# Layers 2 and 3 of a four-layer graph network: attention applied to x first, then the product with W

## What is computed

```python
Wh = jnp.einsum('bnd,de->bne', x, W)
e_src = jnp.einsum('bnd,d->bn', Wh, a_src)
e_dst = jnp.einsum('bnd,d->bn', Wh, a_dst)
logits = e_src[:, :, None] + e_dst[:, None, :]
logits = jnp.where(logits >= 0, logits, 0.2 * logits)
attn = softmax(where(adj == 0, -inf, logits))
out = jnp.einsum('bnm,bmd->bnd', attn, Wh)
```

## Time and profile before

| | us |
|---|---|
| median of 3 runs | 3392.47 (3390.36 to 3393.50) |
| span of the profiled execution | 3390.5 |
| mean granted TensorE clock | 0.992 |
| layer 0 and layer 1, to the start of the last stage | about 2310 |
| last stage | about 1080 |

### The profile page before, as it was taken

How to read it: one execution, slowest core, us unless ns; L and a number is a source line. 1 busy time by engine, 2 the same in 40 slices (tenths; PEclk the granted TensorE clock), 3 DMA queues, 4 the chain that set the end, 5 groups by cost and what they waited for, 6 DMA issues and landing times. The chain is left out here.

```text
span 3390.5 us, 58748 instructions
## 1 busy us (share of the span) xinstructions
PE 3273.9 (97%) x16217; PEld 2651.5 (78%) x16217; DVE 2186.4 (64%) x4753; ACT 1691.7 (50%) x4193; POOL 1989.9 (59%) x2870
## 2 busy tenths in 40 slices
PE   8999989999999999999999999996999999999997
PEld 6777768888888888888888888885777777777775
DVE  6777655555555555555555555555778877877775
ACT  2111135555555555555555555543665666666665
POOL 4555564444444444444444444433888888888886
PEclk9999999999999999999999999998999999999999
DMA  4343310000000000000000000002111111111110
GB/s 140 118 127 126 94 47 16 19 19 19 19 19 19 19 19 19 19 19 19 19 19 19 19 19 19 19 25 90 41 47 56 46 46 56 46 46 50 52 46 28
DMA packets 76527, 143.98 MB, mean 42 GB/s; under 512 B 8640, under 2 KB 8640, under 8 KB 76480
## 3 DMA queue, kind: packets, MB, share of 16 engines
q1 hardware_dynamic: 73920, 135.07, 12.1%
q0 software_dynamic: 2560, 8.39, 0.9%
HBM read 93.09 MB, written 50.33 MB: 42 GB/s over the span
## 5 line engine op out<-in xcount | busy, mean ns | idle before, releaser
L715 POOL TENSOR_TENSOR w_first<-xin,v_row 128x512 f32<-128x512 f32 x512 | 719.9, 1427 | 493.6 <-ACT w_first L753 482.8
L845 DVE TENSOR_TENSOR hT_lo<-hv,hT_hi 128x512 fp32r<-128x512 f32 x256 | 296.7, 1159 | 428.8 <-ACT hT_hi L771 428.8
L47 PE MATMUL whp<-big_hi,xT_hi 128*128 128x512 f32 x1024 | 422.6, 413 | 0.0
L47 PE MATMUL wop<-big_hi,hT_hi 128*128 128x512 f32 x1024 | 405.2, 396 | 0.0
L47 PE MATMUL wop<-big_hi,hT_lo 128*128 128x512 f32 x1024 | 401.0, 392 | 0.0
L47 PE MATMUL whp<-big_lo,xT_hi 128*128 128x512 f32 x1024 | 401.0, 392 | 0.0
L47 PE MATMUL whp<-big_hi,xT_lo 128*128 128x512 f32 x1024 | 400.6, 391 | 0.0
L47 PE MATMUL wop<-big_lo,hT_hi 128*128 128x512 f32 x1024 | 398.7, 389 | 0.0
L767 ACT COPY wh<-whp 128x512 f32<-128x512 f32 x256 | 149.0, 582 | 384.3 <-PE whp L47 384.3
L1139 POOL TENSOR_TENSOR g_terms<-x,g_v_row 128x512 f32<-128x512 f32 x256 | 329.0, 1296 | 5.0 <-ACT x L1219 4.9
L753 ACT ACTIVATE w_first<-w_first 128x512 f32<-128x512 f32 x512 | 319.4, 627 | 5.1 <-POOL w_first L715 5.1
(11 more groups left out here) (200 smaller groups left out, 8018.8 us busy)
## 6 DMA issues: line engine op xcount, KB each, us to landing
xt<-in_x SPq DMA_DIRECT2D x64, 256.0 KB, 2.7
x_scratch<-x SPq DMA_DIRECT2D x64, 256.0 KB, 2.0
xin<-x_scratch SPq DMA_DIRECT2D x64, 256.0 KB, 2.6
att_scratch<-attT SPq DMA_DIRECT2D x64, 256.0 KB, 2.0
att<-att_scratch SPq DMA_DIRECT2D x64, 256.0 KB, 2.7
x1r<-x_scratch SPq DMA_DIRECT2D x64, 256.0 KB, 3.0
out<-res SPq DMA_DIRECT2D x64, 256.0 KB, 2.0
stage<-in_L_gnn_W_heads POOLq DMA_DIRECT2D x16, 256.0 KB, 2.9
```

The costliest lines, as they stand in the source:

```text
L47: ins = nc.tensor.matmul(out, a, b, start=first and c == 0 and q == 0, stop=last and c == n - 1 and q == 2)
L715: nc.gpsimd.tensor_tensor(terms[:, k % TR, :], xin[:], v_row[:, k, :], ALU.mult).then_inc(terms_ready, 1)
L845: nc.vector.tensor_tensor(hT[h % 2][1][:].rearrange("p c n -> p (c n)"), hv[h % 2][:], hT[h % 2][0][:].bitcast(F32).rearrange("p c n -> p ...
```

## The change

For layers 2 and 3, `turn_x`, `sums` and the copy `wh_out` go. `aggregate` takes their place: for each of four chunks of x, an fp32 matmul with the 128x128 chunk of x stationary and `turned` (128 columns) moving. This gives (attn @ x) already transposed, in the bank `agg`. ACT copies its high part (`agg_hi`), DVE makes the low part (`agg_lo`), and `project` multiplies with W and writes straight to `g.sums`, from which `residual` reads. `bank_a` goes, and each layer gets a PSUM bank of its own for scores and turned probabilities. The orders on PE, ACT and DVE are written anew. POOL's and SP's are as before.

PE's order now: `project` g2 (n-3), `pe_turn` g3 (n-4), `spread` g2 (n-2), transposes of `att`, the w1 product, `aggregate` g3 (n-4), transposes of `h1`, `project` g3 (n-4), half of the w2 product, `pe_turn` g2 (n-2), the other half, `spread` g3 (n-3), `aggregate` g2 (n-2).

```diff
@@ ACT @@
-                def x_hi(g, t):
-                    act.wait_ge(g.xT_done, t + 1)
-                    ge(act, g.wh_done, t)
-                    nc.scalar.copy(g.xT[0][:], g.turn[:]).then_inc(g.xT_hi_ready, 1)
-
-                def wh_out(g, t):
-                    act.wait_ge(g.wh_done, t + 1)
+                def agg_hi(g, t):
+                    act.wait_ge(g.agg_done, t + 1)
                     ge(act, g.sums_done, t)
-                    nc.scalar.copy(g.wh[:], bank_a[:]).then_inc(g.wh_ready, 1)
+                    nc.scalar.copy(g.aggS[0][:], g.agg[:]).then_inc(g.agg_hi_ready, 1)
...
-                    if live(n, 2):
-                        wh_out(g2, n - 2)
...
-                    if live(n, 3):
-                        x_hi(g3, n - 3)
+                    if live(n, 4):
+                        agg_hi(g3, n - 4)
...
-                    if live(n, 1):
-                        x_hi(g2, n - 1)
-                    if live(n, 3):
-                        wh_out(g3, n - 3)
+                    if live(n, 2):
+                        turned(g2, n - 2)
+                    if live(n, 4):
+                        ge(act, res_stored, 16 * (n - 4))
+                        normalise(g3.norm, n - 4, g3.z[:], res[:], g3.x_ready)
                     if live(n, 3):
                         g3.att.act_exp(nc, act, n - 3)
                     if live(n, 2):
-                        turned(g2, n - 2)
+                        agg_hi(g2, n - 2)
@@ DVE @@
-                    if live(n, 3):
-                        x_lo(g3, n - 3)
                     if live(n, 4):
-                        residual(g3, n - 4, x3[r % 2][:])
+                        agg_lo(g3, n - 4)
                     if live(n, 0):
...
                     if live(n, 4):
+                        residual(g3, n - 4, x3[r % 2][:])
+                    if live(n, 4):
                         stats(g3, n - 4)
-                    if live(n, 1):
-                        x_lo(g2, n - 1)
...
                     if live(n, 3):
                         peak(g3, n - 3)
+                    if live(n, 2):
+                        agg_lo(g2, n - 2)
+                    if live(n, 3):
                         g3.att.dve_after_exp(nc, dve, n - 3, gate)
@@ PE @@
+                def aggregate(g, t, x):
+                    pe.wait_ge(g.att.turned_ready, 2 * t + 2)
+                    ge(pe, g.agg_lo_ready, t)
                     for c in range(KC):
-                        ins = nc.tensor.transpose(g.turn[:, c, :], x[:, c * P:(c + 1) * P], ident[:])
-                    ins.then_inc(g.xT_done, 1)
+                        ins = nc.tensor.matmul(g.agg[:, c, :], x[:, c * P:(c + 1) * P], g.att.turned[:, 0, :],
+                                               start=True, stop=True)
+                    ins.then_inc(g.agg_done, 1)
...
                 def project(g, t):
-                    pe.wait_ge(g.xT_lo_ready, t + 1)
+                    pe.wait_ge(g.agg_lo_ready, t + 1)
+                    ge(pe, g.z_ready, t)
...
-                    product(nc, bank_a[:], g.xT, (w_hi, w_lo),
-                            [(c, g.q + c) for c in range(KC)]).then_inc(g.wh_done, 1)
+                    product(nc, g.sums[:], g.aggS, (w_hi, w_lo),
+                            [(c, g.q + c) for c in range(KC)]).then_inc(g.sums_done, 1)
...
                 def step(n, r):
+                    if live(n, 3):
+                        project(g2, n - 3)
                     if live(n, 4):
-                        if live(n, 3):
-                            pe.wait_ge(g2.att.turned_ready, 2 * (n - 2))
                         g3.att.pe_turn(nc, pe, n - 4, ident)
                     if live(n, 2):
-                        ge(pe, g3.wh_ready, n - 3)
-                        project(g2, n - 2)
...
                         spread(g2, n - 2)
...
-                    if live(n, 3):
-                        turn_x(g3, n - 3, x3[(r - 3) % 2], g2.x_ready)
                     if live(n, 4):
-                        sums(g3, n - 4)
+                        aggregate(g3, n - 4, x3[r % 2])
...
+                    if live(n, 4):
+                        project(g3, n - 4)
...
+                    if live(n, 3):
+                        spread(g3, n - 3)
                     if live(n, 2):
-                        sums(g2, n - 2)
+                        aggregate(g2, n - 2, x2[(r - 2) % R])
```

More of the change, by code:

```diff
@@ L1042, in __init__ @@
                     self.norm = Norm(nc, ctx, name + "_n", shifted=True)
[L1043 to L1047, removed]
+                    self.agg_done, self.agg_hi_ready, self.agg_lo_ready = (
+                        sem(name + "_agg_done"), sem(name + "_agg_hi_ready"), sem(name + "_agg_lo_ready"))
+                    self.sums_done, self.z_ready, self.x_ready = (
+                        sem(name + "_sums_done"), sem(name + "_z_ready"), sem(name + "_x_ready"))
                     self.diag_v_ready, self.v_spread, self.v_ready, self.terms_ready = (
@@ L1297, in behind, with agg_lo @@
                     weights_lo(k)
[L1299 to L1302, removed]
+                def agg_lo(g, t):
+                    dve.wait_ge(g.agg_hi_ready, t + 1)
+                    nc.vector.tensor_tensor(g.aggS[1][:], g.agg[:], g.aggS[0][:].bitcast(F32), ALU.subtract
+                                            ).then_inc(g.agg_lo_ready, 1)
                 def scores(g, t):
@@ L1409, in _ @@
             def _(pe):
-                def turn_x(g, t, x, ready):
-                    pe.wait_ge(ready, t + 1)
-                    ge(pe, g.xT_lo_ready, t)
+                def aggregate(g, t, x):
+                    pe.wait_ge(g.att.turned_ready, 2 * t + 2)
+                    ge(pe, g.agg_lo_ready, t)
                     for c in range(KC):
-                        ins = nc.tensor.transpose(g.turn[:, c, :], x[:, c * P:(c + 1) * P], ident[:])
-                    ins.then_inc(g.xT_done, 1)
+                        ins = nc.tensor.matmul(g.agg[:, c, :], x[:, c * P:(c + 1) * P], g.att.turned[:, 0, :],
+                                               start=True, stop=True)
+                    ins.then_inc(g.agg_done, 1)
@@ L1424, in spread @@
+                    product(nc, g.sums[:], g.aggS, (w_hi, w_lo),
+                            [(c, g.q + c) for c in range(KC)]).then_inc(g.sums_done, 1)
                 def spread(g, t):
                     pe.wait_ge(g.att.diag_ready, t + 1)
+                    ge(pe, g.att.turned_ready, 2 * t)
                     nc.tensor.matmul(g.att.scores_psum, same_graph[:], g.att.diag[:, 0, :],
                                      start=True, stop=True).then_inc(g.att.scores_done, 1)
-                def sums(g, t):
-                    pe.wait_ge(g.att.turned_ready, 2 * t + 2)
-                    pe.wait_ge(g.wh_ready, t + 1)
-                    ge(pe, g.z_ready, t)
-                    if isinstance(t, int) and t == 0:
-                        pe.wait_ge(g.v_ready, 2)
-                    nc.tensor.matmul(g.sums[:], g.att.turned[:, 0, :], g.wh[:], start=True, stop=True
-                                     ).then_inc(g.sums_done, 1)
@@ L1470, in step @@
                         ins.then_inc(h1T_done, 1)
-                    if live(n, 1):
-                        turn_x(g2, n - 1, x2[(r - 1) % R], x2_ready)
-                    if live(n, 3):
-                        ge(pe, g2.wh_ready, capped(n - 1, T))
-                        project(g3, n - 3)
-                        if live(n, 2):
-                            pe.wait_ge(g2.att.summed, n - 1)
-                        elif live(n, 4):
-                            pe.wait_ge(g3.att.turned_ready, 2 * (n - 3))
-                        spread(g3, n - 3)
+                    if live(n, 4):
+                        project(g3, n - 4)
                     if live(n, 0):
@@ L1486, in step @@
                     if live(n, 2):
-                        if live(n, 3):
-                            pe.wait_ge(g3.att.summed, n - 2)
                         g2.att.pe_turn(nc, pe, n - 2, ident)
```

34 lines of the change are left out of this document (13 added, 21 removed).

## The result

| | before | after |
|---|---|---|
| median of the runs, us | 3392.98 (3390.36 to 3394.24, 4 runs) | 3908.43 (3898.58 to 3913.81, 4 runs) |
| ratio | | 1.1515, 95% interval 1.1498 to 1.1532 |
| span of the profiled execution, us | 3390.5 | 3912.1 |
| mean granted TensorE clock | 0.992 | 0.933 |
| one step, mean from 2600 to 3200 us | 16.00 | 23.99 |

The direction was forecast, the size was not: 3755 us was predicted, with 3630 to 3840 as range, and the time lies 68 us above that. A step grew by 7.99 us instead of 5.85. Of the 522 us between the two spans, 487 lie between the first and the last of DVE's 64 adds for y (2336.87 to 3340.75 us before, 2342.66 to 3833.55 after), 6 ahead of the first and 29 behind the last.

What follows compares the result with a forecast made beforehand. A PE and DVE ring of 16.05 us a step was taken as the bound. New waits made it 20.5: 62 x 4.45 = 276 us, plus clock 62 x 1.4 = 87, gave 3755 us, range 3630 to 3840.

Steps and rivals of the forecast that it cites:

- spread g3 to project g2: End of step: from spread through g3's exponential, then g2's high and low halves and semaphore, to project g2; 3.05 us.
- residual to h1 add: DVE's list from residual of g2 through norm of y, z1, scores and gate to h1's add; 7.43 less 0.13, 7.3 us.
- h1 add to project g3: Middle of step: h1 add to low half 0.60, low half 0.68, semaphore 0.06; 1.35 us.
- The first uncovered wait: End of step: PE has nothing between aggregate of g2 and project g2 while ACT and DVE make halves; idles 2.1 us.
- The second: DVE's residual of g2, second in its list, must wait for project g2's output; all of DVE's list stands behind it.
- 4.0 us that PE was to idle in one piece: Mid-step, ahead of h1's turns: PE has 7.1 us of work from project g2's start, turns can start at 11.1.
- The step that failed is the term for the clock: Half clock behind the 4.0 us middle idle stretch: 1.4 us a step, 0 and 2.5 as ends; 87 us over 62 steps.
- 2.43 us stretch: Idle stretch in the earlier kernel's last 47 us, behind which the clock stayed 1.00; cited against loss behind the 2.1 us gap.
- the ring: Chain of waits through PE, ACT and DVE setting each step: 20.5 us predicted, 4.45 more than 16.05.
- clock lost twice a step: Rival: clock also lost behind the 2.1 us gap, project g2 at half speed; 62 x (4.45 + 2.5), 3823 us; chance 0.10.
- no clock loss: Rival: idle stretches short enough, or placed so that the clock holds; 62 x 4.45, 3668 us; chance 0.25.
- PE's saving: PE's two turn_x and two sums replaced by two aggregates: 1.0 us a step at most, 0.8 without the transpose that stays.

Runs made afterwards that it cites:

- e1: Changed kernel plus extra matmuls nobody reads on PE, 8 behind the aggregate of g2 and 10 behind that of g3: 3737 us, ratio 1.1017.
- e4: e1 with 2 instead of 10 middle matmuls, residual of g2 behind its peak on DVE, its POOL and ACT followers behind norm 1: 3590 us.
- e5: e1 with ACT's copy of the high part of g3 ahead of norm 1 instead of behind it: 3684 us, ratio 1.0872.
- e6: e1 with POOL's low part of att behind the probabilities of g3 instead of ahead: 3706 us, ratio 1.0937.
- v4: Changed arithmetic, all lists rewritten, project g2 split on PE, a POOL add moved to DVE, POOL reordered, norm 3 one step later: 3378 us, ratio 0.9962.
- e3: Changed kernel with only the 10 extra matmuls behind the aggregate of g3, in the middle of the step: 3778 us, ratio 1.1137.
- e8: Changed kernel with extra matmuls in both gaps, 4 and 5 of them instead of 8 and 10: 3771 us, ratio 1.1121.

## Why the prediction was wrong

The two new waits and their ring were named rightly, and the cost of the clock was mispriced. The terms of the prediction's sum, and what one step of the changed kernel (3212.01 to 3236.15) and one of e1, at full clock (3003.59 to 3024.62), show:

| term, us | forecast | changed kernel | e1 |
|---|---|---|---|
| spread g3 to project g2 | 3.05 | 3.61 | 3.61 |
| project g2 to residual | 3.05 | 4.64 | 3.11 |
| residual to h1 add | 7.3 | 6.29 | 6.29 |
| h1 add to project g3 | 1.35 | 2.27 | 2.27 |
| project g3 and w2 product, to spread g3 | 5.75 | 7.33 | 5.75 |
| sum | 20.5 | 24.14 | 21.03 |
| clock, a term of its own in the forecast | 1.4 | in the rows above | none |

So the clock has 1.5 us in each project and 3.1 us in this step.

The first uncovered wait was right: PE idles 2.33 us ahead of project g2, 2.1 forecast. The second was right: DVE waits 3.79 us for project g2's sums, and e4 shows what that is worth. Of the 4.0 us that PE was to idle in one piece ahead of the turns of h1, 2.72 came, and 3.0 at full clock (from the end of the aggregate to the turns in e1), because the h1 add came earlier.

The step that failed is the term for the clock. I took 1.4 us a step, where the runs show 2.9 on average from 2600 to 3200 us (changed kernel against e1) and 3.1 in the step shown. I argued that "the work on both sides is denser" and that only the middle stretch would lose the clock, because 2.1 us is under the 2.43 us stretch that kept it. That stretch was no bound. The row read for it, 3380 to 3382 us, ends before PE works again, and behind the stretch PE had only one transposition and one product of g3, no project that could have become slow. In the changed kernel the clock was lost at both places in 19 of 25 steps, behind 2.33 us and behind 2.72 and 0.87 us in the step shown, with dense work on both sides. I also set a part of the loss beside DVE's work, in the turns of h1; but there the clock is still 1.00, and the loss falls on the two projects, which are on the ring.

The rival "clock lost twice a step" had the mechanism, and it had been given 0.10. Its 3823 us are too low because it took 2.5 us for both losses together, on a ring of 20.5. The rival "no clock loss" is answered by e1, which took 3737 us where 3668 was forecast.

Two smaller errors add to this. At full clock the mean step is 21.1 us, 0.6 more than the sum. And the count of 62 steps gave the ends too little: the last add for y is followed by 78.6 us instead of 49.8. Of the 153 us between 3755 and 3908, 62 x 2.14 = 133 come from the longer step (1.5 us of clock and 0.6 us of ring); the other 20 are what the ends take beyond 62 full steps.

That the ring at full clock missed by so little is in part luck, since two of its terms were wrong in opposite ways. Rows of the kernel before:

```profile
2979.91 1.18 DVE L151 TENSOR_TENSOR g_inv<-g_inv,gate 128x1 f32<-128x1 f32 x1
```

```profile
2979.78 2.53 POOL L1139 TENSOR_TENSOR g_terms<-x,g_v_row 128x512 f32<-128x512 f32 x2
```

```profile
2979.93 0.81 ACT L1219 ACTIVATE x<-z,n_shift,n_rstd 128x512 f32<-128x512 f32 x1 [0.25 <-POOL n_shift L227]
2980.65 0.56 ACT L1197 CAST g_xT_hi<-turn 128x512 fp32r<-128x512 f32 x1
```

Residual to h1 add came out 1.0 us shorter: in the kernel before, DVE's gate multiply of g2 starts 0.13 us behind the start of POOL's terms of g3 and takes 1.18 us; in the changed kernel both start at 3222.86 and it takes 0.16. I had priced the stretch as it stood. h1 add to project g3 came out 0.9 us longer, for the same reason: ACT's copy of g3 stands behind norm 1 in both kernels, 7.07 us after the residual before and 7.19 now. Before, the h1 add was late enough to hide it; with the add 1.0 us earlier the copy is what project g3 waits for. So the residual to project g3 takes 8.56 us where 8.65 was forecast. e5, which moves the copy, gets 0.8 us of this back.

Spread to project came out 0.56 us longer: the scores of g3 moved beside POOL's low part of att, and the leaky step lasts until that ends (3209.84 and 3209.77); e6 gives 0.5 back. This is the 0.5 us by which the step of e1 exceeds the sum.

The range failed for the same reason as the forecast. Its upper end, 64 steps x (4.45 + 2.5), had the clock's cost of one stretch only once; with the 2.5 of the earlier trace rows at both places it would have been about 3997 us, and it would have held the time.

PE's saving was as forecast in the order of the changed kernel: from an aggregate of g3 to the first extra matmul in e1 are 0.80 us, against 0.81 in the earlier trace rows, and the step of e1 without its 1.8 us of idle time and 4.6 us of extra matmuls leaves 14.6 us of work, against 15.4 before (16.05 less 0.62). In v4 it is 14.9, so a part of the saving is gone; there project g2 is cut into three pieces, but what the cuts cost was not tried alone. Whether v4's 0.4% come from the arithmetic or from its orders is open too: the orders of v4 were not tried on the arithmetic of the kernel before.

## What to carry to other kernels

Taking work off the busiest engine pays only if its order still has something to do between each result and its next use; write down, for each new dependence, what stands between producer and consumer on every engine, and what is queued behind a wait on an in-order engine. Price idle time on PE twice, once as itself and once as the half clock of the work that follows, at every gap and not only at the longest, and take a gap that once kept the clock as no proof that the next will. When an operation moves in a list, look at what it will now lie beside and behind on the other engines, since its duration and the readiness of its source both come from there.

## What the runs showed of the hardware

Filling idle stretches with products that nobody reads made a kernel 4.4% faster (3908 to 3737 us). Idle stretches of 2.4 and 2.5 us lost the clock in one step and kept it in the next (e3), and with none over 1.6 us it was still lost in every third step (e8). Where it is lost, it falls late: at one place 1.00 through the idle stretch and the turns behind it, then 0.51 in the project; at the other 0.63 from 3235.80 to 3236.10 us, the last 0.3 us ahead of the project.

The Trainium skill (TensorE: Matmul & The Clock Gate, Terms) prices the loss as throttled time x (1 - K/N), where K/N is the share of clock pulses let through. An estimate by that rule for a step of the changed kernel is 0.15 x 24.0 = 3.6 us, while e1 won 2.9 us in the same stretch of time. The rule counts slow idle time too (at 3235.80 to 3236.10, ahead of project g2, the clock is already 0.63); whether that is all of the difference was not worked out.

DVE's short operations with both inputs in SBUF last until POOL's 128x512 operation ends, if that began first: the leaky step of g3 0.75 us beside one and 0.22 without (e6), the gate multiply about 1.2 us beside one and 0.16 where both start together. The h1 add, which reads one input from PSUM, takes its usual 0.69 us beside POOL's terms (3222.94). The Trainium skill (SBUF — State Buffer, SBUF: two separate sides) says that a VectorE instruction with two SBUF inputs and a GpSimd instruction that reads SBUF hold their shared ports exclusively, whichever starts first, for the whole instruction; the durations agree.
